# A four-stage transformer kernel: biases carried by a constant 128th feature instead of matmuls, with loads, gathers and combines moved

## What is computed

```python
ln = lambda x: (x - x.mean(-1)) / sqrt(x.var(-1) + eps)          # no gain, no offset
# A: 8 experts, best 2 by ctx @ Wg + bg, softmax weights
x += sum_e comb[:, e] * (relu(ln(x) @ W1[e] + b1[e]) @ W2[e] + b2[e])
# B: 16 experts in 4 groups of 4; best 2 groups, best 4 experts in them, by sigmoid(ln(x) @ Wg.T)
x += sum_e w[:, e] * ((silu(ln(x) @ W1[e].T + b1[e]) * (ln(x) @ W3[e].T + b3[e])) @ W2[e].T + b2[e])
# C: attention of ln(x) on ctx, 16 heads of 8, causal mask
# D: ln with gain and offset, 128 -> 512 -> 128 with int32 weights, silu, residual
```

## Time and profile before

| | |
|---|---|
| median of 3 runs | 892.51 us (890.3 to 893.62) |
| profiled execution, own time | 897.39 us |
| its span, first to last instruction | 895.6 us |
| PE busy | 789.7 us (88%), mean granted clock 0.966 |
| DVE, ACT, POOL busy | 632.5, 503.6, 395.8 us |
| DMA | 104.60 MB, mean 117 GB/s |
| ahead of stage A's first tile | 0 to 44.6 us |
| stage A's tiles | 44.6 to 298.5 us |
| stage B's tiles, first and second half | 298.5 to 440, 440 to 581 us |
| stages C and D | 581 to 896 us |

### The profile page before, as it was taken

One profiled execution on the slowest core, in us unless ns is written; L12 is line 12 of the kernel. 1 busy time (PEld: TensorE's weight loads), 2 busy tenths in 40 slices (PEclk: granted clock), 3 DMA queues, 4 the chain that ended last, 5 costly groups with the idle time before them and its releaser, 6 DMA issues.

```text
span 895.6 us, 18099 instructions
## 1 busy us (share of the span) xinstructions
PE 789.7 (88%) x5521; PEld 604.2 (67%) x5576; DVE 632.5 (71%) x1888; ACT 503.6 (56%) x976; POOL 395.8 (44%) x460
## 2 busy tenths in 40 slices
PE   3499889998988899998799899878999998998897
PEld 3478778787987687876688688645555555554675
DVE  6868544466569477779667566588888888885786
ACT  2545455565754557775366466534555555555786
POOL 6335774077000777500467740046766443445100
PEclk9999899998999899999899899989999999999899
DMA  9394377773112228202115220124455445441011
GB/s 308 117 332 135 124 237 198 232 223 110 51 49 80 68 66 334 74 22 77 42 56 146 69 61 13 58 76 123 127 148 141 130 112 161 111 118 48 12 36 48
DMA packets 96156, 104.60 MB, mean 117 GB/s; under 512 B 13401, under 2 KB 71145, under 8 KB 94780
## 3 DMA queue, kind: packets, MB, share of 16 engines
q1 hardware_dynamic: 79106, 80.77, 29.0%
q0 software_dynamic: 8608, 18.22, 8.1%
q10 hardware_dynamic: 8352, 4.46, 1.7%
HBM read 67.17 MB, written 36.23 MB: 115 GB/s over the span
## 4 chain that ended last, share of the span: by engine, by line
PE 53%; DVE 17%; POOL 10%; issue 7%; DMA 7%; ACT 3%; SPq 2%; DVEq 0%; POOLq 0%; ACTq 0%
PE y_ps L2038 4%; POOL yg L664 3%; PE y_ps L1951 3%; PE hid_ps L2014 3%; PE y_ps L1822 3%; PE hid_ps L1936 3%; PE hid_ps L2015 2%; PE hid_ps L2026 2%; PE tr_ps L2097 2%; DMA v_rows<-sg 2%; PE hid_ps L1919 2%; POOL yg L642 2%; PE tr_ps L2069 2%; PE hid_ps L1810 2%; POOL xr L634 1%
## 5 line engine op out<-in xcount | busy, mean ns | idle before, releaser
L634 POOL DMA_INDIRECT xr<-b_tokens,idx_sb x70 | 67.2, 960 | 122.1 <-DVE idx_sb L891 101.9
L1113 DVE TENSOR_TENSOR hl<-hid_ps,hh 128x512 fp32r<-128x512 f32 x78 | 53.8, 690 | 61.3 <-ACT hh L1503 60.7
L1280 DVE TENSOR_REDUCE negmax<-hid_ps 128x4 f32<-128x512 f32 x128 | 85.8, 683 | 12.0 <-PE hid_ps L2015 11.6
L1822 PE MATMUL y_ps<-region,hh 128*128 x312 | 86.1, 353 | 8.0 <-DVE hl L1113 7.8
L642 POOL DMA_INDIRECT yg<-a_rows,idx_a x64 | 61.6, 963 | 53.2 <-PE cb_ps L1899 34.1
L664 POOL DMA_INDIRECT yg<-b_rows,idx_b x64 | 61.8, 965 | 43.7 <-DMA b_rows<-yo 26.3
L1497 ACT ACTIVATE zb<-hid_ps 128x512 f32<-128x512 f32 x78 | 46.4, 595 | 57.5 <-PE hid_ps L1802 57.5
L1227 DVE TENSOR_TENSOR zb<-hid_ps,sg 128x256 f32<-128x256 f32 x70 | 29.7, 424 | 66.7 <-ACT sg L1590 41.2
L1584 ACT ACTIVATE sg<-hid_ps 128x512 f32<-128x512 f32 x70 | 41.7, 596 | 61.4 <-PE hid_ps L1921 61.3
L2015 PE MATMUL hid_ps<-region 128*128 128x512 f32 x128 | 75.6, 592 | 0.0
L1951 PE MATMUL y_ps<-region,hh 128*128 x280 | 74.7, 344 | 0.6 <-DVE hl L1238 0.6
(11 more groups left out here) (344 smaller groups left out, 2394.7 us busy)
## 6 DMA issues: line engine op xcount, KB each, us to landing
region<-k_strips SPq DMA_DIRECT2D x128, 64.0 KB
region<-k_strips SPq DMA_DIRECT2D x32, 256.0 KB, 2.9
region<-hl SPq DMA_DIRECT2D x128, 64.0 KB, 2.0
k_strips<-k_halves SPq DMA_DIRECT2D x24, 256.0 KB, 4.7
region<-nought SPq DMA_DIRECT2D x6, 1024.0 KB, 13.1
a_rows<-yo SPq DMA_DIRECT2D x20, 256.0 KB
b_rows<-yo SPq DMA_DIRECT2D x18, 256.0 KB
staged<-a_w_in SPq DMA_DIRECT2D x16, 256.0 KB, 6.8
```

The costliest lines, as they stand in the source:

```text
L634: g.indirect_dma_start(xr[:, q % 3, j * RB:j * RB + w], None, src, bass.IndirectOffsetOnAxis(ap=rows.bitcast(U32), axis=0)).then_inc(x_got ...
L1280: v.tensor_reduce(negmax[:, s % 2, b, :], hid_ps[b % 2][:].rearrange("p (i k) -> p i k", i=HG), AX, ALU.max, negate=True).then_inc(c_max, 1)
L1822: t.matmul(y[:, c0:c0 + 2 * P], hh[:, n % 2, cs], w2a[:, bass.ds(e * (2 * FA) + c * 2 * P, 2 * P)], start=c == 0, stop=False)
```

## The change

**Bias as a feature.** As the normed features of a token sum to zero, the last one is minus the sum of the others. The kernel after writes only 127 normed features and keeps the constant 1 in the last column of `wide`. The weights become W[i] - W[127] for i < 127, and row 127 becomes the bias. `up_a` and `up_b` lose their bias matmuls; `down_a` keeps that of `b2`.

**Stage A's weights** are folded at the start: the row of `b1` is loaded into partition 127 of `staged` (one DMA of 16 KB), PE multiplies each of the 8 raw pieces by `less_last` (the identity with -1 in row 127), and ACT copies 127 rows of the product over a place in `staged` before it splits them.

**Stage B's weights.** The host puts `b1` and `b3` in row 127 and gives the removed rows as `b_last`. For each of the 8 pieces of W1 and W3 (`FOLD`, k = 20 to 27) a second DMA brings 512 values of `b_last`, repeated over 127 partitions, into `rt`, and DVE subtracts it a step before the split. `W2` is now split first. From k = 18 on, ACT requests the pieces, two steps after the split that frees the buffer.

**Order.** `store_kv` comes ahead of `store_rows`; the blocks of ctx are taken in the order `KVB` = 4, 5, 0, ... and `gather_a(0)` waits for 6 of the 8; `gather_slots(5)` moves ahead of two powers and `scatter_a(4)`; in the second half of stage B the slots' gathers go ahead of each `gather_b`, and `CMB2` goes from (4, 7, 10, 13) to (6, 13, 18, 23).

```diff
-        KVB = (6, 7, 0, 1, 2, 3, 4, 5)
+        KVB = (4, 5, 0, 1, 2, 3, 6, 7)
-        CMB2 = (4, 7, 10, 13)
+        CMB2 = (6, 13, 18, 23)
...
+        FOLD = range(NRAW_A + EB // EQ, NRAW_B)
...
+        def fold_buf(k):
+            return staged[:, (NRAW_A + k) * BT:(NRAW_A + k + 1) * BT]
+        def last_row(k):
+            return rt[0:P - 1, raw_slot(k) * BT:(raw_slot(k) + 1) * BT]
...
@@ SP @@
+            sp.dma_start(staged[P - 1:P, NRAW_A * BT:], a_b1).then_inc(in_last, 16)
             sp.wait_ge(bias_split, 1)
-            sp.dma_start(brow[:, 0:AW].rearrange("k (p j) -> p k j", p=P), bias16[:, :, 0:AW // P]).then_inc(bias_out, 16)
...
+            sp.dma_start(brow.rearrange("k (p j) -> p k j", p=P), bias16).then_inc(bias_out, 16)
...
-            sp.dma_start(brows[0:3, :], brow[:, 0:AW]).then_inc(bias_in, 16)
-            sp.dma_start(brows[3:6, :], brow2).then_inc(bias_in, 16)
-            sp.dma_start(brows[6:9, 0:EA * P], brow[:, AW:]).then_inc(bias_in, 16)
+            sp.dma_start(brows[6:9, 0:EA * P], brow).then_inc(bias_in, 16)
...
+                for i in range(NB):
+                    if 4 * q < VAT[i] + 2 <= 4 * q + 4:
+                        store_kv(i)
                 store_rows(q)
                 for i in range(NB):
                     if 4 * q < VAT[i] + 2 <= 4 * q + 4:
-                        store_kv(i)
...
-                while nraw < NRAW_B and split_step(nraw - 2) < 4 * q + 4:
-                    load_raw(nraw)
-                    nraw += 1
...
@@ POOL @@
+            step(g.affine_select(out=less_last, in_=ident[:], compare_op=ALU.not_equal, fill=-1.0, base=1 - P,
+                                 pattern=[[0, P]], channel_multiplier=1))
+            g.memset(wide[:, :, :, P - 1:P], 1.0)
...
-                if b == 0:
-                    pool.wait_ge(kv_mm, 2 * NB)
+                if b < 2:
+                    pool.wait_ge(kv_mm, 2 * NB - 4 + 4 * b)
...
             gather_slots(4)
+            gather_slots(5)
             power(6, 7)
             power(7, 8)
             scatter_a(4)
-            gather_slots(5)
...
+            gather_slots(QA + GB + 3)
             gather_b(0)
+            gather_slots(QA + GB + 4)
+            gather_slots(QA + GB + 5)
             gather_b(1)
-            gather_slots(QA + GB + 3)
+            gather_slots(QA + GB + 6)
             gather_b(2)
-            gather_slots(QA + GB + 4)
+            gather_slots(QA + GB + 7)
             gather_b(3)
...
@@ DVE @@
+                    if n == split_step(k) - 1 and k in FOLD:
+                        eng.wait_ge(in_raw[raw_slot(k)], raw_landed(k))
+                        rows = raw_buf(k)[0:P - 1, :]
+                        v.tensor_tensor(rows, rows, last_row(k), ALU.subtract).then_inc(b_folded, 1)
...
@@ ACT @@
-            for k in range(8):
+            eng.wait_ge(in_last, 16)
+            for k in range(EA):
+                eng.wait_ge(fold_mm, k + 1)
+                a.activation(fold_buf(k)[0:P - 1, :], hid_ps[k % 4][0:P - 1, :], ACT.Copy).then_inc(folded, 1)
+                eng.wait_ge(folded, k + 1)
                 split_high(k)
...
+                for k in range(NRAW_A + 2, NRAW_B):
+                    if n == split_step(k - 2) + 2:
+                        eng.wait_ge(raw_lo[lo_engine(k - 2)], lo_count(k - 2))
+                        a.dma_start(raw_buf(k), raw_src[k][0]).then_inc(in_raw[raw_slot(k)], 16)
+                        if k in FOLD:
+                            row = b_last[:, (k - FOLD.start) * BT:(k - FOLD.start + 1) * BT]
+                            a.dma_start(last_row(k), bass.AP(row.tensor, row.offset, [[0, P - 1], [1, BT]])).then_inc(in_raw[raw_slot(k)], 16)
...
@@ PE @@
+            def fold(k):
+                eng.wait_ge(in_raw[raw_slot(k)], raw_landed(k))
+                if k >= 4:
+                    eng.wait_ge(folded, k - 3)
+                t.matmul(hid_ps[k % 4][:], less_last, raw_buf(k), start=True, stop=True).then_inc(fold_mm, 1)
             logits(0)
+            for k in range(EA):
+                fold(k)
             eng.wait_ge(chosen, 1)
             prefix(EA, 0)
...
-                t.matmul(z, pick[:, 0, :], brows[:, bass.ds(e * FA, FA)], start=True, stop=False)
-                t.matmul(z, xTh[:, q % 2, js], w1h[:, bass.ds(e * FA, FA)], start=False, stop=False)
+                t.matmul(z, xTh[:, q % 2, js], w1h[:, bass.ds(e * FA, FA)], start=True, stop=False)
...
-                t.matmul(z, pick[:, 1, :], brows[:, bass.ds(e * BT, BT)], start=True, stop=False)
...
-                t.matmul(z, pick[:, 1, :], brows[:, bass.ds(e * BT + BW, BT)], start=True, stop=False)
```

More of the change, by code:

```diff
@@ L48, with build @@
 NS = 2
-def build(nc, x, ctxT, first, early, c_kv, c_ones, a_w1, a_w2, b_w1, b_w3, b_w2, late, b_b2, c_w, d_fc1, d_fc2, d_scales, out):
+def build(nc, x, ctxT, first, early, c_kv, c_ones, a_w1, a_b1, a_w2, b_w1, b_w3, b_last, b_w2, late, b_b2, c_w, d_fc1, d_fc2, d_scales, out):
     with ExitStack() as ctx:
@@ L78, in build @@
         region1 = sb("region1", [P, 4 * EA * FA], F32R)
-        with nc.sbuf_tensor("staged", [P, 16 * BT], F32) as staged:
+        with nc.sbuf_tensor("staged", [P, 24 * BT], F32) as staged:
             pass
@@ L152, in build @@
         ah, al = (part(region2, 6 + k, BT) for k in range(2))
-        k_hi, k_lo = ([part(region2, 20 + 2 * k + w, BT) for k in range(2)] for w in range(2))
+        k_hi, k_lo = ([part(region2, 10 + 4 * w + k, BT) for k in range(2)] for w in range(2))
         fc1h, fc1l = part(region2, 8, BT), part(region2, 9, BT)
@@ L205, in build @@
         raw_hi, raw_lo = sem("raw_hi"), [sem(f"raw_lo{k}") for k in range(2)]
+        in_last, fold_mm, folded = sem("in_last"), sem("fold_mm"), sem("folded")
+        b_folded = sem("b_folded")
         bias_split, bias_out, bias_in = sem("bias_split"), sem("bias_out"), sem("bias_in")
@@ L322, in build @@
         EQ = BT // P
+        for q in range(EB // EQ):
+            v = w2b[:, q * 2 * BT:(q + 1) * 2 * BT].rearrange("p (c s d) -> p c s d", c=EQ, s=2)
+            raw_src.append((b_w2[:, q * BT:(q + 1) * BT], v[:, :, 0, :], v[:, :, 1, :]))
         for src, wh, wl in ((b_w1, bw1h, bw1l), (b_w3, bw3h, bw3l)):
@@ L340, in raw_buf @@
             return staged[:, k * BT:(k + 1) * BT] if k < NRAW_A else raw[:, raw_slot(k), :]
+        def fold_buf(k):
+            return staged[:, (NRAW_A + k) * BT:(NRAW_A + k + 1) * BT]
         def raw_landed(k):
             last = max(k + 1, k // 4 * 4 + 4) if k < NRAW_A else k + 1
-            return 16 * sum(raw_slot(m) == raw_slot(k) for m in range(last))
+            return sum(16 * (1 + (m in FOLD)) for m in range(last) if raw_slot(m) == raw_slot(k))
+        def last_row(k):
+            return rt[0:P - 1, raw_slot(k) * BT:(raw_slot(k) + 1) * BT]
         def lo_engine(k):
@@ L352, in raw_view @@
         def raw_view(k):
[L353 removed]
+            v, like = (fold_buf(k) if k < EA else raw_buf(k))[:, 0:raw_src[k][0].shape[1]], raw_src[k][1]
             return v if len(like.shape) == 2 else v.rearrange("p (c d) -> p c d", c=like.shape[1])
@@ L1447, in split_high @@
                 eng.wait_ge(in_raw[raw_slot(k)], raw_landed(k))
+                if k in FOLD:
+                    eng.wait_ge(b_folded, k - FOLD.start + 1)
                 a.activation(raw_src[k][1], raw_view(k), ACT.Copy).then_inc(raw_hi, 1)
@@ L1917, in up_b @@
                 z = hid_ps[0][:]
-                t.matmul(z, pick[:, 1, :], brows[:, bass.ds(e * BT, BT)], start=True, stop=False)
-                t.matmul(z, xTh[:, r, js], bw1h[:, bass.ds(e * BT, BT)], start=False, stop=False)
+                t.matmul(z, xTh[:, r, js], bw1h[:, bass.ds(e * BT, BT)], start=True, stop=False)
                 t.matmul(z, xTl[:, r, js], bw1h[:, bass.ds(e * BT, BT)], start=False, stop=False)
@@ L1924, in up_b @@
                 z = hid_ps[1 + m % 2][:]
-                t.matmul(z, pick[:, 1, :], brows[:, bass.ds(e * BT + BW, BT)], start=True, stop=False)
-                t.matmul(z, xTh[:, r, js], bw3h[:, bass.ds(e * BT, BT)], start=False, stop=False)
+                t.matmul(z, xTh[:, r, js], bw3h[:, bass.ds(e * BT, BT)], start=True, stop=False)
                 t.matmul(z, xTl[:, r, js], bw3h[:, bass.ds(e * BT, BT)], start=False, stop=False)
```

54 lines of the change are left out of this document (25 added, 29 removed).

## The result

The changed kernel takes 915.45 us (median of 4 runs, 914.42 to 916.03); the kernel before, run beside it, 891.92 us. The ratio is 1.0262, 95% interval [1.024, 1.0285]. The profiled execution took 916.03 us, its span is 914.3 us (before 895.6), PE's granted clock 0.930 (before 0.966). The forecast was 887.5 us and the range ended at 907. Only rival 2 pointed this way, and its 904 to 907 are too low as well.

The account below looks back on a forecast made before the run. PE was taken to set the pace, with DMA engines to watch beside stage A. -23.5 - 8.3 + 4 + 28 - 6 + 1 = -4.8 on the profiled 897.4 gave 892.6, less 4.9 to the median, said as 887.5 us; range 846 to 907.

Parts of the forecast that it names:

- rival 2: Stage A, steps 13 to 46: the loaded engine takes 156 us, not 136, up to +45; time 904 to 907; chance 0.18.
- start: Ahead of stage A: folding the weights on PE and ACT delays the first gather and tables; +4 us (1 to 6).
- steps 13 to 46: Stage A while stage B's weights load: 127-row loads on one engine make 136 us of 108; +28 us (0 to +45).
- stage A outside them: Stage A outside steps 13 to 46: 44 removed bias matmuls at 0.21 us, 0.9 of it; -8.3 us.
- stage B, matmuls and order: Stage B: removed bias matmuls bring -23.5 us, the reordered gathers of the second half -6 us.
- token gathers; stages C and D: End of each half of stage B: tokens are gathered while shorter steps go by; +1 us.
- large unknown: Stage A, steps 13 to 46: how a load of 127 rows is dealt to the 16 engines; one engine taken, +28 us.
- rival 1: Stage A, steps 13 to 46: the 127-row loads are spread or one engine keeps up; -18 for +28; time 847; chance 0.24.
- I take 0.8 of 29.4 us: -23.5: Stage B: 0.8 of the 29.4 us of removed bias matmuls is gained, as DVE's waits shrink with PE's work.
- both stalls and part of the half clock that follows as gone: -6: Stage B's second half: slots first and later `CMB2` remove DVE's waits for slots and row gathers; -6 us (-2 to -8).
- rival 3: Stage B: DVE becomes the bound and only half of 29.4 us comes; +9 us, time 896; chance 0.10.
- First `up_a` at 48 to 49: Start of stage A: sign that the first tile starts at 48 to 49 us instead of 44.6.

Follow-up runs that it names:

- e1: The changed kernel with the repeated row loaded over 128 partitions in place of 127; 876.36 us, ratio 0.9784 to the kernel before.
- e2: The changed kernel with POOL's old order of gathers and old `CMB2` in stage B's second half; 915.44 us, ratio 1.0209.
- e3: The changed kernel with both the load of e1 and the order of e2; 873.17 us, ratio 0.9747.
- e18: The changed kernel with 16 of POOL's gathers for blocks 4 to 7 left out, part of the result not computed; 913.23 us, ratio 1.019.
- e17: The changed kernel itself, run again unchanged beside e18; 914.33 us, ratio 1.0211.
- e14: The kernel of e13 with stage B's 140 bias matmuls put back, adding rows of zeros; 1062.95 us.
- e5: The changed kernel with the repeated row loaded by two DMAs, of 122 and 5 rows, in place of one of 127; 879.57 us, ratio 0.98.
- e13: The changed kernel with e1's load and POOL's power moved ahead of `gather_b(3)`, same kernel as e7 on another chip; 1042.64 us, ratio 0.9712.
- e7: The changed kernel with e1's load and POOL's power moved ahead of `gather_b(3)`; 1042.72 us, ratio 0.9756.
- e8: The kernel of e7 with `gather_a(7)` ahead of the slots of group 5 in stage B's first half; 1044.58 us, ratio 0.9754.
- e9: The same kernel as e7 on another chip; 1045.87 us, ratio 0.9741.

## Why the prediction was wrong, step by step

From the profiled executions, the sum was -4.8 us and +18.7 came (895.6 to 914.3).

| term | predicted | measured |
|---|---|---|
| start | +4 | +2.1 |
| steps 13 to 46 | +28 | +28.5 |
| stage A outside them | -8.3 | -2.5 |
| stage B, matmuls and order | -23.5 and -6 | -6.7 |
| token gathers; stages C and D | +1 | -2.7 |

**The large unknown was read rightly.** One engine for 127 rows (the completions), 136 us for the window (136.5), DVE's wait in front of the subtraction and `low_a` behind it, and e1 for the other side: with the load spread, the window is 18.0 us shorter than before, which is the -18 of rival 1; the two waits of PE that it counted (4.8 and 4.24 us) are absent from e1's trace, and the window's granted clock is 1.00 for 0.95. That 136 was met to half a microsecond is luck, though: the sum of the engine's work gave 156, and the step down from it had a reason but no row. Rival 1's 847 would still not have come: e1's span is 872.0, because the rest of its sum was the forecast's.

**The step that failed is "I take 0.8 of 29.4 us: -23.5", together with "both stalls and part of the half clock that follows as gone: -6".** Between `up_b` 0 and 69 the kernel before takes 272.3 us and the changed one 265.6. e2 and e3 part the two terms: the matmuls alone bring 6.9 and 8.0 us in place of 23.5, and the new order on top nothing in place of 6 (265.6 for e2's 265.4; in e1, 267.7 for e3's 264.3). The prediction held that PE sets the pace of stage B and looked for another bound at DVE alone. It never priced POOL's row of gathers, which runs without a gap, or with one of 5 us, beside 41 of the 69 steps. Rival 3 let half of the 29.4 us come and named DVE; under a third came, and POOL held most of the rest:

- `up_b` 0 to 18 takes 69.9 us for 70.3. e18 shows that POOL's row holds it.
- 18 to 35, where POOL does little, 74.2 for 75.6. This is rival 3, below.
- 35 to 58, 89.9 for 90.8. The table under e2 has POOL's row end at the same place whatever the order; that it is the bound is read from the traces, not tested.
- 58 to 69, behind the row, 31.7 for 35.6. Only these 11 tiles bring about their price, 3.9 of 4.4 us.

The same by steps, against the clean price:

- At the clean price 69 tiles lose 69 x 0.40 = 27.6 us.
- The order did remove both stalls: the steps 48, 51 and 52 take 9.1 us for 17.5, 7.2 more than the clean price. Taken alone that is the -6.
- The late power took it back, and more: step 57 takes 15.97 us for 3.15, 13.2 lost against the clean price. The prediction followed the gathers that were moved forward and not the instruction that stands behind all of them in POOL's queue. The kernel before had it done only 0.7 us ahead of its use, so a stage that reaches it earlier must wait.
- Steps 18 to 35 give 1.4 of 6.8 us. This is rival 3, in one quarter of stage B. DVE is busy for 59.08 of 74.20 us there. Its waiters, in the kernel before and in the changed one:

```profile
PEld hid_ps L1936 <- DVE zb L1230: 6.2, 4, 2.6
...
PE hid_ps L1936 <- DVE hl L1238: 5.0, 6, 2.2
```

```profile
PEld hid_ps L1968 <- DVE zb L1244: 13.3, 8, 3.2
...
PE hid_ps L1968 <- DVE hl L1252: 10.1, 8, 2.8
```

  PE's matmul work fell by 6.4 us (64.44 to 58.08), and its wait for DVE's `hl` grew by 5.1, that of its weight loads for `zb` by 7.1. The prediction had looked at DVE's share of halves, 85% and 68%. The routing work is tied to certain steps, and some of these even got longer: steps 19, 25 and 31 take 5.0, 5.7 and 7.3 us for 4.4, 5.3 and 6.5. That DVE's work is what holds them is read from these waits; no run took it out.
- Step 14 takes 9.67 us for 5.35, 4.7 lost, to POOL's row of gathers (e18).
- These make -11.5. The other 4.8 us are spread over steps such as 11, 13, 35, 54 and 58, which the runs don't explain singly.

The same error at stage A's scale: 44 x 0.21 x 0.9 should have been 44 x 0.15 at best, 6.6, and 2.5 came (a second profile of the same kernel, e17, has up_a 48 to 77 at 89.1 us for 91.0, so this term carries 2 us of scatter). The start was mis-sized only: ACT's chain decided, but POOL's first gather came 2.4 us later and the first tile 2.1, not 4. In the profiled executions the sum is off by 23.5 us. The median is 27.7 us off (915.45 for 887.7) because I took off 4.9 us for the step from profile to median, and the changed kernel's profile lies only 0.6 above its median.

**Of the signs named.** Window, one completion for each FOLD load, no wait for `v_rows` or `b_rows`: right. First `up_a` at 48 to 49: 46.7. Tiles 2.07 and 2.73 apart: 2.13 and 2.75. The range's upper end, 907, came from rival 2 alone. It held stage B's gain fixed while the window varied; with the window as forecast and most of stage B's gain gone the time is 915. Missing was the case in which both unfavourable terms hold.

**Left open.** The matmuls were put back by themselves only on the other chips (e14, 20.3 us); on a chip of the first group e2 and e3 stand in for that, with one profile each. Whether moving the power ahead of the last gathers pays there, and whether fewer gathers would free the second half of stage B, was not run. How the clock's share of each loss divides was not separated from the waits that go with it.

## What to carry to other kernels

The row count of a DMA requested by ACT decided over its engines: pad 127 rows to 128 or cut them into 122 and 5, and count completions in the queue's packets to see which it was. Price a removed instruction by stretches in which its engine is the bound, step by step where background work is tied to steps, and not by an engine's mean share over half a stage. Look for a queue whose idle time is nothing but issues, as POOL's was: the steps tied to it take the time of its row, whatever PE saves. Reordering such a queue moves the wait and doesn't shorten the row. When it is done all the same, list what stands behind the moved work, with its first waiter; here a power of 1.7 us came 12.7 us late.

## What the runs showed of the hardware

- DMAs from ACT's queue of 128, 127, 122 and 5 rows had 16, 1, 2 and 5 completions (the last two as a sum of 7 a pair, e5); SP's of 3 rows 3.
- A gather of POOL's in a row of them took 0.95 us and 0.30 to the next. 60 of them, with one wait of 5 us, put the instruction behind them 82.4 to 83.0 us after `up_b(35)` in the five kernels of the table under e2.
- The first matmul of a tile takes 0.31 us to the next one where it follows `down_a` directly, and the slot of a matmul ahead of it was worth only 0.15 us of its 0.23.
- The same kernel takes 892 to 897 us on some chips and 1070 to 1073 on others, four fifths of the difference between e3's span and e13's in the three stretches where POOL gathers most (`up_a` 15 to 48, `up_b` 0 to 18 and 35 to 54); the ratios of the remedied kernels (e1, e3, e5, e7, e8, e9, e13) to it are 0.971 to 0.980 on both, and leaving 16 gathers out there saves 20 us of a stretch where it saves 5.9 here.
